# Shifts of two layer norms moved from ScalarE to GpSimd, with a new order of statistics and variances

## What is computed

```python
def _layernorm(x, axis=-1, eps=1e-05):
    m = jnp.mean(x, axis=axis, keepdims=True)
    v = jnp.var(x, axis=axis, keepdims=True)
    return (x - m) / jnp.sqrt(v + eps)
...
        def step(carry, qkv):
            S, z = carry
            qt, kt, vt = qkv
            S = S + jnp.einsum('bhd,bhe->bhde', kt, vt)
            z = z + kt
            num = jnp.einsum('bhd,bhde->bhe', qt, S)
            den = jnp.einsum('bhd,bhd->bh', qt, z)[..., None] + EPS
            return ((S, z), num / den)
...
    x = x + _L0_attn_ref(_layernorm(x, axis=-1), L0_attn_wq, ...)
    x = x + _L0_xattn_ref(_layernorm(x, axis=-1), ctx_1024, ctx_1024, ...)
    x = x + _L0_ffn_ref(_layernorm(x, axis=-1), L0_ffn_norm_scale, ...)
```

## Time and profile before

| | us |
|---|---|
| median of 3 runs | 626.69 |
| lowest and highest | 625.57, 626.8 |
| profiled execution | 626.32 |
| its span in the trace | 624.1 |
| busy in the span: PE, DVE, ACT, POOL | 556.2, 504.1, 417.6, 407.6 |

### The profile page before, as it was taken

One profiled execution on the slowest core, in us unless ns is written; L12 is line 12 of the kernel. 1 busy time (PEld: TensorE's weight loads), 2 busy tenths in 40 slices (PEclk: granted clock), 3 DMA queues, 4 the chain that ended last, 5 costly groups with the idle time before them and its releaser, 6 DMA issues.

```text
span 624.1 us, 16569 instructions
## 1 busy us (share of the span) xinstructions
PE 556.2 (89%) x4286; PEld 407.8 (65%) x4287; DVE 504.1 (81%) x1506; ACT 417.6 (67%) x1188; POOL 407.6 (65%) x459
## 2 busy tenths in 40 slices
PE   4888999999999998878899786899999999999993
PEld 1333444444444444445888544799999999999993
DVE  4489999999999999874578988466887878877883
ACT  3556878888888775532888502445887888878882
POOL 2778888888888888112877501764566766757762
PEclk9979999999999999899999969999999999999998
DMA  5510111111161112362568480221111111111110
GB/s 153 187 50 2 35 35 36 35 34 34 34 101 34 34 37 65 67 137 57 159 196 206 78 137 5 59 51 38 35 50 51 47 44 47 52 40 51 52 45 22
DMA packets 49973, 40.99 MB, mean 66 GB/s; under 512 B 21971, under 2 KB 40278, under 8 KB 49926
## 3 DMA queue, kind: packets, MB, share of 16 engines
q1 hardware_dynamic: 44150, 29.68, 19.5%
q0 software_dynamic: 4960, 10.49, 6.4%
q10 hardware_dynamic: 816, 0.26, 0.2%
HBM read 27.54 MB, written 12.88 MB: 65 GB/s over the span
## 4 chain that ended last, share of the span: by engine, by line
PE 55%; ACT 16%; DVE 10%; issue 10%; POOL 4%; DMA 3%; ACTq 0%; SPq 0%; DVEq 0%; POOLq 0%
PE bank L1349 30%; PE run L1349 19%; ACT xh L678 4%; PE bank L1353 4%; ACT xs L780 2%; ACT ex L656 2%; DMA shared<-xs_d,row_u 2%; ACT nb_a L675 2%; PE run L1616 1%; ACT ex L661 1%; DVE mean_early L1057 1%; ACT xT L649 1%; PE run L1540 1%; DMA ct<-in_ctx_r 1%; ACT rl L657 1%
## 5 line engine op out<-in xcount | busy, mean ns | idle before, releaser
L616 POOL DMA_INDIRECT shared<-xs_d,row_u x91 | 87.8, 965 | 62.6 <-DVE row_u L1247 31.6
L549 POOL TENSOR_TENSOR shared<-v,qk 128x1024 f32<-128x1024 f32 x64 | 125.0, 1953 | 2.8
L623 POOL DMA_INDIRECT out_x<-shared x64 | 63.5, 992 | 48.2 <-DVE shared L1319 22.1
L899 DVE TENSOR_TENSOR R<-run,qk 128x1024 f32<-128x1024 f32 x64 | 77.5, 1210 | 12.5 <-PE run L1349 11.0
L1349 PE MATMUL bank<-wqkv,xT 128*64 128x128 f32 (+1 forms) x384 | 70.5, 353 | 15.5 <-ACT v L659 10.8
L1349 PEld LDWEIGHTS bank<-wqkv,xT 128*64 128x64 f32 (+1 forms) x384 | 33.4, 159 | 72.1 <-issue 37.4
L909 DVE TENSOR_REDUCE num<-R 128x128 f32<-128x1024 f32 x64 | 77.2, 1206 | 1.1
L1349 PE MATMUL run<-shared,tris_s 64*64 64x512 f32 x512 | 73.3, 644 | 0.0
L809 ACT ACTIVATE shared<-run,scale_s 128x128 f32<-128x128 f32 (+1 forms) x78 | 30.0, 385 | 41.5 <-PE run L1616 41.5
L540 POOL TENSOR_TENSOR qk<-ex,rl 128x256 f32<-128x256 f32 x64 | 46.5, 727 | 11.0 <-DVE mv_a L884 7.5
L656 ACT ACTIVATE ex<-bank 128x256 f32<-128x256 f32 x64 | 24.1, 376 | 28.9 <-PE bank L1349 28.9
(11 more groups left out here) (277 smaller groups left out, 1425.1 us busy)
## 6 DMA issues: line engine op xcount, KB each, us to landing
xs_d<-xs SPq DMA_DIRECT2D x16, 270.0 KB, 5.2
X<-in_x SPq DMA_DIRECT2D x16, 256.0 KB, 2.7
ct<-in_ctx_t SPq DMA_DIRECT2D x16, 256.0 KB, 3.0
ct<-in_ctx_r SPq DMA_DIRECT2D x16, 256.0 KB, 3.7
gram_d<-gd SPq DMA_DIRECT2D x14, 256.0 KB, 2.4
w_s<-in_w_experts SPq DMA_DIRECT2D x8, 384.0 KB, 3.9
circ<-prob_d SPq DMA_DIRECT2D x30, 64.0 KB, 2.8
shared<-xs_d,row_u POOLq DMA_INDIRECT x91, 2.6
```

Source lines behind the costliest of these rows:

```text
L549: nc.gpsimd.tensor_tensor(outer[k].rearrange("p (h e d) -> p h e d", h=H, e=D), vv.unsqueeze(3).broadcast_to([P, H, D, D]), kk.unsqueeze(2 ...
L616: nc.gpsimd.indirect_dma_start(xg[q], None, xs_d[:, :], bass.IndirectOffsetOnAxis(ap=rows, axis=0)).then_inc(xg_in[q], 16)
L623: nc.gpsimd.indirect_dma_start(out[:, :], bass.IndirectOffsetOnAxis(ap=xg[(NXI + j) % NX][:, DEST:DEST + 1].bitcast(U32), axis=0), yg[q], ...
L899: nc.vector.tensor_tensor(R[:, 0:D * E].rearrange("p (h e d) -> p h e d", h=H, e=D), run[k % 2][:].rearrange("p (h e d) -> p h e d", h=H, ...
```

## The change

Four edits, in the attention pipeline only.

1. ACT no longer makes the negated means and the shifts. `negative_mean` is gone, and `norm` waits for a shift that is ready and only writes the rows.
2. POOL makes the shift of four tiles in two instructions of 128x4, `mean_times_root` and `shift`. For group a0 both stand behind its root; for group c they are made one slot later, when it is d: the product behind the first features, the shift behind the first outer product.
3. POOL's order changes. Variance and root of a0 move behind the third features; variance and root of c move behind the fourth features and the fourth outer product.
4. DVE's order changes. The statistics of a0 are taken ahead of the key products and the moments right behind them; X is added behind the third sum, the statistics of c are taken behind the fourth product and its moments behind the fourth sum. In the last slot DVE waits for POOL's shift and makes none of its own.

```diff
+            def mean_times_root(g, p, mv, rs, rs_sem, mr, mr_sem, nb_sem):
+
+                pool.wait_ge(rs_sem, g + 1)
+                need(pool, nb_sem, g)
+                nc.gpsimd.tensor_tensor(mr[:], mv[p][:, :, 0], rs[p][:], ALU.mult).then_inc(mr_sem, 1)
+
+            def shift(g, p, mr, mr_sem, nb, nb_sem, normed):
+
+                pool.wait_ge(mr_sem, g + 1)
+                need(pool, normed, GT * (g - 1))
+                settle(pool)
+                nc.gpsimd.tensor_scalar(nb[p][:], mr[:], -1.0, 1.0, ALU.mult, ALU.add).then_inc(nb_sem, 1)
+
...
                 if a1:
                     features(*a1, 0)
+                if d:
+                    mean_times_root(d[0], d[1], mv_c, rs_c, c_rs, mr_c, c_mr, c_nb)
+                if a1:
+                    outer_product(*a1, 0)
+                if d:
+                    shift(d[0], d[1], mr_c, c_mr, nb_c, c_nb, d_xh)
+                if a1:
+                    features(*a1, 1)
+                    outer_product(*a1, 1)
+                    features(*a1, 2)
                 if a0:
                     variance(*of_a)
-                if a1:
-                    outer_product(*a1, 0)
-                    features(*a1, 1)
                 if a0:
                     root(*of_a)
-                if a1:
-                    outer_product(*a1, 1)
-                    features(*a1, 2)
-                if c:
-                    variance(*of_c)
+                    mean_times_root(a0[0], a0[1], mv_a, rs_a, a_rs, mr_a, a_mr, a_nb)
+                    shift(a0[0], a0[1], mr_a, a_mr, nb_a, a_nb, a_xh)
                 if a1:
                     outer_product(*a1, 2)
                     features(*a1, 3)
                 if c:
-                    root(*of_c)
+                    variance(*of_c)
                 if a1:
                     outer_product(*a1, 3)
+                if c:
+                    root(*of_c)
...
-            def norm(g, p, rs, rs_sem, mr, mr_sem, nb, nb_sem, dst, dst_sem, own=GT):
-                act.wait_ge(rs_sem, g + 1)
-                act.wait_ge(mr_sem, g + 1)
+            def norm(g, p, rs, nb, nb_sem, dst, dst_sem, own=GT):
+                act.wait_ge(nb_sem, g + 1)
                 for k in range(own):
-                    nc.scalar.activation(nb[p][:, k:k + 1], mr[:, k:k + 1], ACT.Copy, bias=1.0, scale=rs[p][:, k:k + 1]).then_inc(nb_sem, 1)
-                for k in range(own):
-                    act.wait_ge(nb_sem, GT * g + k + 1)
                     nc.scalar.activation(dst[:, k, :], X[:, bass.ds(GT * g + k, 1), :].rearrange("p a b -> p (a b)"),
                                          ACT.Identity, bias=nb[p][:, k:k + 1], scale=rs[p][:, k:k + 1]).then_inc(dst_sem, 1)
...
                     quotients(*c)
+                if a0:
+                    g, p, r = a0
+                    dve.wait_ge(x_in[p], 16 * r + 16)
+                    stats(g, p, st_a, a_st, mv_a, a_mv, a_mr, 1)
                 if b:
                     key_dots(*b)
                 if a0:
-                    g, p, r = a0
-                    dve.wait_ge(x_in[p], 16 * r + 16)
-                    stats(g, p, st_a, a_st, mv_a, a_mv, a_nb, GT)
+                    moments(a0[0], a0[1], st_a, a_st, mv_a, a_mv, a_mr, 1)
                 if b:
                     sum_heads(*b, 1)
                     sum_dots(*b)
...
                 if b:
                     times_q(*b, 2)
+                    sum_heads(*b, 2)
                 if c:
                     add_attention(*c)
                 if b:
-                    sum_heads(*b, 2)
+                    times_q(*b, 3)
                 if c:
                     dve.wait_ge(c_x1, c[0] + 1)
-                    stats(c[0], c[1], st_c, c_st, mv_c, c_mv, c_nb, GT)
-                if b:
-                    times_q(*b, 3)
-                if c:
-                    moments(c[0], c[1], st_c, c_st, mv_c, c_mv, c_nb, GT)
+                    stats(c[0], c[1], st_c, c_st, mv_c, c_mv, c_mr, 1)
                 if b:
                     sum_heads(*b, 3)
+                if c:
+                    moments(c[0], c[1], st_c, c_st, mv_c, c_mv, c_mr, 1)
```

More of the change, by code:

```diff
@@ L146, in build @@
         xh2 = sb("xh2", [P, GT, E])
-        last_mr = sb("last_mr", [P, GT // 2])
         x2T, k2T = sb("x2T", [P, GW]), sb("k2T", [P, GW])
@@ L271, in build @@
         gram_out = sems("gram_out", 2)
-        last_nb = sem("last_nb")
         diag_in, mean_ch, mean_mm, prob_e = sem("diag_in"), sem("mean_ch"), sem("mean_mm"), sem("prob_e")
@@ L553, in slot @@
             def slot(n, i):
-                a0, a1, c = stage(n, i, 2), stage(n, i, 1), stage(n, i, -1)
+                a0, a1, c, d = (stage(n, i, k) for k in (2, 1, -1, -2))
                 of_a = a0 and (a0[0], a0[1], mv_a, a_mv, ve_a, a_ve, rs_a, a_rs, a_xh)
@@ L665, in denominators @@
                 nc.scalar.activation(den[:], den[:], ACT.Copy, bias=ATT_EPS).then_inc(c_den, 1)
-            def negative_mean(g, p, mv, mv_sem, mr, mr_sem):
-                act.wait_ge(mv_sem, GT * g + GT)
-                nc.scalar.activation(mr[:], mv[p][:, :, 0], ACT.Copy, scale=-1.0).then_inc(mr_sem, 1)
-            def norm(g, p, rs, rs_sem, mr, mr_sem, nb, nb_sem, dst, dst_sem, own=GT):
-                act.wait_ge(rs_sem, g + 1)
-                act.wait_ge(mr_sem, g + 1)
+            def norm(g, p, rs, nb, nb_sem, dst, dst_sem, own=GT):
+                act.wait_ge(nb_sem, g + 1)
                 for k in range(own):
-                    nc.scalar.activation(nb[p][:, k:k + 1], mr[:, k:k + 1], ACT.Copy, bias=1.0, scale=rs[p][:, k:k + 1]).then_inc(nb_sem, 1)
-                for k in range(own):
-                    act.wait_ge(nb_sem, GT * g + k + 1)
                     nc.scalar.activation(dst[:, k, :], X[:, bass.ds(GT * g + k, 1), :].rearrange("p a b -> p (a b)"),
@@ L690, in slot @@
                     a_evac_xT(*a1)
-                if d:
-                    negative_mean(d[0], d[1], mv_c, c_mv, mr_c, c_mr)
                 if a1:
@@ L703, in slot @@
                     need(act, d_tr, g)
-                    norm(g, p, rs_c, c_rs, mr_c, c_mr, nb_c, c_nb, xh2, d_xh, GT // 2 if i is None and g == NG - 1 else GT)
+                    norm(g, p, rs_c, nb_c, c_nb, xh2, d_xh, GT // 2 if i is None and g == NG - 1 else GT)
                 if d:
@@ L717, in slot @@
                     need(act, a_tr, g)
-                    negative_mean(g, p, mv_a, a_mv, mr_a, a_mr)
-                    norm(g, p, rs_a, a_rs, mr_a, a_mr, nb_a, a_nb, xh, a_xh)
+                    norm(g, p, rs_a, nb_a, a_nb, xh, a_xh)
                 if a1:
@@ L965, in slot @@
             def slot(n, i):
-                a0, a1, b, c = (stage(n, i, s) for s in (2, 1, 0, -1))
+                a0, b, c = (stage(n, i, k) for k in (2, 0, -1))
                 if b:
@@ L986, in slot @@
                     sum_dots(*b)
-                if a0:
-                    moments(a0[0], a0[1], st_a, a_st, mv_a, a_mv, a_nb, GT)
                 if i is None and n == FIRST:
@@ L1031, in last_rows @@
             def last_rows(g, p):
[L1032 to L1038, removed]
+                dve.wait_ge(c_nb, g + 1)
                 dve.wait_ge(d_tr, g)
```

## The result

The changed kernel takes 668.01 us (median of 4 runs, 665.68 to 669.11) against 626.13 for the kernel before (4 runs): a ratio of 1.0672, 95% interval 1.0629 to 1.0715. It is 42 us slower. The profiled execution is the fastest of the four. It took 665.68 us, a span of 663.9, which is 39.8 more than before.

The account below looks back on a forecast made before the run. The prediction took a loop through PE and ACT, 14.81 us a slot, as the bound; 626.3 + 22.1 (twelve slots of longer chain and later xh2) + 9.6 (clock falls) = 658.0, forecast 658 us, range 646 to 669.

Parts of the forecast that it names:

- that case: The forecast itself: a wait in each full slot with some falls of the clock, 652 to 662 us, chance 0.49.
- a fall of the clock in every slot: Rival: PE's clock falls in all twelve slots, 667 us (662 to 670), chance 0.2.
- The step that carried it: On POOL, the variance-to-shift block behind the third features makes ACT's xh wait; the loop grows by 1.71 us per slot.
- The chain: From ACT's third exponential through POOL's features, variance, root, product and shift to ACT's xh: 2.80 us against 1.09 before.
- The term of the signal to POOL: From the end of ACT's third exponential to the start of POOL's features: 0.05 us.
- The shift for xh2: On POOL behind the first outer product; it makes xh2 and its transposes 0.13 us later in each slot.
- The walk: POOL's steps from the start of a slot to the end of the shift for xh2, summed to 8.12 us.
- The clock: PE's longer gap before the transposes lowers its clock in two of three slots: 8 x 1.2 = 9.6 us.
- my inference from three gaps: From PE gaps of 2.30, 1.56 and 1.69 us: a 2.0 us gap lies nearer to a fall of the clock.
- Head and tail: The three slots ahead of the twelve full ones, and the last shift on POOL in the tail, were costed at nothing.
- no falls: Rival: the wait without any fall of PE's clock, 649 us (646 to 652), chance 0.25.
- The rival in which ACT's work comes back: Faster if shift follows the third exponential by less than 1.09 us: slots near 14.4 us, 622 us, chance 0.04.

Follow-up runs that it names:

- kernel 2: The kernel before with one edit: variance and root of the group two ahead stand behind the third features on POOL; 661.13 us, ratio 1.0533.
- (5): The changed kernel with variance and root of the group two ahead behind the second features, product and shift left behind the third; 640.87 us, ratio 1.0223.
- kernel 1: The changed kernel with variance, root, product and shift of the group two ahead behind the second features instead of the third; 622.3 us, ratio 0.9937.
- (3): The changed kernel with DVE's order of before; 667.97 us, ratio 1.0672.
- kernel 10: From kernel 1: POOL makes only the shift of xh, ACT that of xh2, DVE the last rows', with DVE's order of before; 617.18 us, ratio 0.9835.
- 11: kernel 10 with the first half of DVE's new order: statistics ahead of the key products, moments right behind them; 615.68 us, ratio 0.9817.
- kernels 6: kernel 1 with the shift for xh2 moved ahead of the first outer product on POOL; 623.14 us, ratio 0.9961.
- 7: kernel 1 with the shift for xh2 ahead of the first outer product, and DVE's order of before; 622.55 us, ratio 0.9949.

## Why the prediction was right

The time lies in the range, 646 to 669, but 1 us below its upper end. It is 10 us above the 658 that I called likeliest and outside the 652 to 662 of that case: the growth was 42 us where the sum had 31.7. The number falls in the band of a rival, a fall of the clock in every slot (662 to 670), whose condition did not hold. So the mechanism was right, and that the number stayed in the range is partly luck.

**The step that carried it held.** The block behind the third features sits on the loop; the wait is on ACT, for nb_a, twelve times; order alone reproduces 33 of the 42 us (kernel 2), a shorter chain gives a shorter wait (5), and one tile earlier removes it (1). DVE's order hides behind the long slot (3).

**The chain was undersized: 3.18 us, not 2.80.** The term of the signal to POOL was 0.24, not 0.05: I had taken it from ACT to PE. Product to shift was 0.42, not 0.29: the pair in the earlier trace rows ends with a shift that has one scalar and, in the code, no increment of `settled` ahead of it; which of the two counts was not tried. And shift to ACT was 0.15 instead of 0.05; the shift itself, 0.19, was below its 0.23.

**The shift for xh2 cost 0.34 us a slot, not 0.13.** ACT started xh2 at 8.36 us of the slot (169.54 - 161.18) against my 8.12, and PE's transposes came at 10.07 instead of 9.73. The walk itself was right within 0.05 us: the shift ended at 169.35, which is 8.17. It left out the signal from there to ACT, 0.19. Chain and xh2 together are 2.09 + 0.34 = 2.43 us, and the slot shown is 17.26 - 14.81 = 2.45 longer. On average over the twelve it is 17.34 - 14.82 = 2.52, so 30 us where I had 22.1.

**The clock was right in size by luck.** I had 9.6 us, by a fall of 1.2 us in two slots of three. Keeping PE at work gave back about 11 (7.2 between the profiled executions). But there were fewer falls, and dearer ones. In the profile eight of the twelve gaps of 2.2 to 2.5 us were followed by full speed. This is PE around one of them:

```profile
225.45 0.66 PE L1352 MATMUL bank<-id_s,xh 128*128 128x128 f32 x4 [0.39 <-ACT xh L687]
...
229.53 0.69 PE L1348 MATMUL bank<-x2T,k2T 128*64 128x64 f32 x16
232.72 0.65 PE L1352 MATMUL bank<-id_s,xh 128*128 128x128 f32 x4 [2.50 <-ACT xh L687]
233.31 1.09 PE L1348 MATMUL run<-shared,tris_s 64*64 64x512 f32 x8
```

Four slots held a fall and took 18.7, 17.8, 18.1 and 19.6 us instead of 17.3, that is 0.4 to 2.3 us each, 4.7 together; another fell at the head of the tail. The first of the four fell in a gap of 2.98 us ahead of its slot, so it is none of the twelve. A gap of 2.50 us is longer than the 2.30 of the earlier trace rows and went unpunished, so the length of a gap alone does not decide, and my inference from three gaps did not hold.

**Head and tail were not free.** Transposes at 54.60 answer to 53.30 before: 1.3 us. From the last ones of the loop to the end it is 396.6 us against 393.0: 3.6 us. Of these, 3.1 lie ahead of the last X. In kernel 1, whose clock held over the first 20 us behind those transposes (1.00, against 0.66 in the first 10 after the change), that stretch is 0.8 us longer than before: so some 2.3 us are that fall's. The 0.8 are not taken apart; the clock falls in kernel 1, too, a little later. From the last X to the reduction mean_early it is 5.66 us instead of 5.03, in kernels 1 and 3 as well, of which 3 has DVE's old order, and 5.02 in kernel 10, where DVE makes its own last shift: the shift on POOL in the last slot costs 0.6 us where I had put nothing. Accounts: 212.7 - 177.9 = 34.9 us in twelve slots (30 of wait, 5 of clock), 1.3 ahead, 3.6 behind; together 39.8.

**Of the rivals**, no falls gave 649, and a fall in every slot 667. The measured time is near the latter for another reason: a longer wait with fewer falls. The rival in which ACT's work comes back did not come about here, since the shift follows the exponential by far more than 1.09 us. In kernels 10 and 11 its condition holds (ACT does not wait for nb_a), and their slots of 14.33 us are near its 14.4. The Trainium skill ("GPSIMD Engine Reference", section 4.1) would keep elementwise work on VectorE and calls GpSimd about twice as slow for two inputs. At this size the trace does not show that factor: the product of 128x4 took 0.20 us on POOL, as in the earlier trace rows, and DVE's own of half the size, 128x2, 0.16 us in the last slot before (268.82). No run has the product of 128x4 on DVE. The 0.2 us that the prediction would add by the factor are no further term, since the 0.20 us in its sum was measured on POOL. The fastest kernels have one shift on POOL; what the engine's full list costs showed with both (kernels 6 and 7).

## What to carry to other kernels

Before an instruction is moved on an engine that executes in order, write down what the one ahead of it waits for, and who waits for the one behind: here four small operations got a signal of ACT's in front of them and ACT behind them. That place alone cost 33 of the 42 us, with two of the operations and no work added; all four add no more than 0.8 us of work a slot. Price a chain across engines by rows with the same pair of engines, and with the same dependence on the instruction just ahead; the sum of durations was an eighth too small (2.80 for 3.18 us). Give each signal on the way a term, the last one too. When several edits come together, split them: one of these (POOL's shift of xh, placed a tile earlier) belongs to the fastest kernels, one (the second half of DVE's order) is a loss in short slots, and the place of the variance hid both.

## What the runs showed of the hardware that was not expected

- An idle POOL started its features 0.24 us after ACT's instruction ends (173.56 to 173.80).
- What an instruction of POOL idles when it waits for the one just ahead depends on the pair: 0.22 us from product to shift (189.38 + 0.20 to 189.80), but 0.08 from variance to root (174.80 to 174.88) and from root to product (175.90 to 175.98).
- Gaps of 2.43 to 2.50 us on PE, the same from slot to slot, were followed by 2.4 GHz in some slots and by 1.2 GHz in others.
